# Router matmuls with the high and low weights side by side in one 32-column stationary operand

## The reference, cut to what matters

```python
logits = jnp.einsum('bsd,ed->bse', hidden_states, gate_w)      # 512 x 256 by 16 x 256, in each batch
scores = jax.nn.softmax(logits, axis=-1).transpose(0, 2, 1)
topk_w, topk_idx = jax.lax.top_k(scores, cap)                  # cap = 64 tokens of each expert
...
g = jnp.einsum('becd,efd->becf', x_tok, Wg)
u = jnp.einsum('becd,efd->becf', x_tok, Wu)
h = jax.nn.gelu(g, approximate=False) * u
eo = jnp.einsum('becf,edf->becd', h, Wd) * topk_w[..., None]
...
shared = jnp.einsum('bsf,df->bsd', jax.nn.gelu(gs, approximate=False) * us, Ws_d)
```

## Time and profile before

| | |
|---|---|
| time, median of 3 runs | 2467.9 us (2467.69 to 2471.45) |
| span of the profiled execution | 2465.3 us |
| phase A, to the last router matmuls | about 1268 us of it |
| TensorE busy | 96% |
| VectorE busy in phase A, by slices of the page | mostly 6 to 8 tenths |

### The profile page before, as it was taken

One profiled execution on the slowest core, in us unless ns is written; L12 is line 12 of the kernel. 1 busy time (PEld: TensorE's weight loads), 2 busy tenths in 40 slices (PEclk: granted clock), 3 DMA queues, 4 the chain that ended last, 5 costly groups with the idle time before them and its releaser, 6 DMA issues.

```text
span 2465.3 us, 40995 instructions
## 1 busy us (share of the span) xinstructions
PE 2372.3 (96%) x14388; PEld 2086.3 (85%) x14388; DVE 1567.9 (64%) x3198; ACT 1032.8 (42%) x1912; POOL 1150.4 (47%) x997
## 2 busy tenths in 40 slices
PE   6999999999998999999987999999999999999997
PEld 5888888888887888888876888888888888888886
DVE  6677767778776877788846455555554545555553
ACT  3545545444553545545442333333333333333332
POOL 1233333333332333333352666666666666666664
PEclk9999999999998999999998999999999999999999
DMA  2111111111111111111115444443444444434433
GB/s 90 53 44 59 51 60 60 52 51 57 54 61 44 60 43 60 52 60 60 59 62 90 86 90 82 88 84 66 79 84 87 86 85 88 84 60 86 84 62 43
DMA packets 78506, 167.03 MB, mean 68 GB/s; under 512 B 11744, under 2 KB 46720, under 8 KB 78368
## 3 DMA queue, kind: packets, MB, share of 16 engines
q0 software_dynamic: 49152, 67.14, 16.7%
q1 hardware_dynamic: 29216, 97.85, 11.8%
HBM read 97.71 MB, written 67.24 MB: 67 GB/s over the span
## 4 chain that ended last, share of the span: by engine, by line
PE 84%; DVE 6%; issue 4%; POOL 2%; DMA 1%; ACT 1%; SPq 0%; DVEq 0%; POOLq 0%; ACTq 0%
PE ps L349 26%; PE ps L351 26%; PE ps L350 26%; PE ps L501 2%; DVE stage L856 2%; PE ps L387 1%; DVE bn_stats L758 1%; PE ps L420 1%; DMA stage<-in_wd 1%; DVE x_t L753 1%; PE ps L442 1%; DVE hidden L753 1%; POOL rstd L1144 1%; POOL out L1209 1%; ACT x_t L693 0%
## 5 line engine op out<-in xcount | busy, mean ns | idle before, releaser
L349 PE MATMUL ps<-x_t,weights 128*128 128x512 f32 x1536 | 617.3, 402 | 23.2 <-DVE hidden_f L1111 13.3
L350 PE MATMUL ps<-x_t,weights 128*128 128x512 f32 x1536 | 602.5, 392 | 0.0
L351 PE MATMUL ps<-x_t,weights 128*128 128x512 f32 x1536 | 601.8, 392 | 0.0
L1209 POOL DMA_INDIRECT out<-x_rows,step_token x256 | 418.1, 1633 | 333.9 <-DVE x_rows L1090 275.4
L349 PE MATMUL ps<-weights,hidden 128*128 128x256 f32 x1536 | 435.8, 284 | 8.7 <-POOL hidden L1148 5.6
L351 PE MATMUL ps<-weights,hidden 128*128 128x256 f32 x1536 | 436.1, 284 | 0.0
L350 PE MATMUL ps<-weights,hidden 128*128 128x256 f32 x1536 | 436.0, 284 | 0.0
L1111 DVE TENSOR_TENSOR hidden_f<-gelu,ps 128x512 f32<-128x512 f32 x256 | 175.7, 686 | 379.0 <-ACT gelu L733 348.1
L733 ACT ACTIVATE gelu<-ps 128x512 f32<-128x512 f32 x256 | 152.8, 597 | 535.8 <-PE ps L351 508.4
L349 PEld LDWEIGHTS ps<-x_t,weights 128*128 128x128 f32 x1536 | 290.6, 189 | 83.6 <-DVE hidden_f L1111 13.5
L1148 POOL TENSOR_TENSOR hidden<-hidden_f,hidden 128x512 fp32r<-128x512 f32 x128 | 165.5, 1293 | 408.7 <-ACT hidden L647 408.7
(11 more groups left out here) (174 smaller groups left out, 4436.9 us busy)
## 6 DMA issues: line engine op xcount, KB each, us to landing
x_rows<-in_x SPq DMA_DIRECT2D x32, 512.0 KB, 3.5
pairs<-mod_rows SPq DMA_DIRECT2D x32, 512.0 KB, 4.3
h_rows<-stage SPq DMA_DIRECT2D x32, 512.0 KB, 2.6
out<-y_rows SPq DMA_DIRECT2D x32, 512.0 KB, 2.9
stage<-in_wg SPq DMA_DIRECT2D x16, 512.0 KB, 3.4
stage<-in_wd SPq DMA_DIRECT2D x16, 512.0 KB, 4.4
stage<-in_wu SPq DMA_DIRECT2D x16, 512.0 KB
x_rows<-h_rows,step_token POOLq DMA_INDIRECT x256
```

The lines of the kernel that those rows point to most:

```text
L349: pe.matmul(o, lhs(HI), rhs(HI), start=start, stop=False)
L350: pe.matmul(o, lhs(HI), rhs(LO), start=False, stop=False)
L351: return pe.matmul(o, lhs(LO), rhs(HI), start=False, stop=stop)
L1209: pool.indirect_dma_start(out=out_rows, out_offset=bass.IndirectOffsetOnAxis(ap=ICUR[g][:, t:t + 1], axis=0), in_=X1[:, g % 2, t * D:(t + ...
```

## The change

The router weights are laid out so that the 16 HI and the 16 LO columns of one half of the features are neighbours. One matmul with these 32 stationary columns gives HI weights by HI rows in PSUM rows 0 to 15 and LO weights by HI rows in rows 16 to 31; a second one with the 16 HI columns adds HI weights by LO rows to rows 0 to 15. There are four router matmuls a batch in place of six. The logits' copy and the four transposes then carry 32 rows, and VectorE adds the two groups with a reduction of its own into a new SBUF tile `GLS`, waits for it, and takes the maximum and the difference from `GLS`, not from PSUM.

```diff
--- before.py
+++ after.py
@@ -69,7 +69,7 @@
         V = sb("v", [P, 2, T, D], F32R)
         ROTK = sb("rot_k", [P, 2, KD, P], F32R)
         ROTV = sb("rot_v", [P, 2, KD, P], F32R)
-        GW = sb("gate_w", [P, 2, KD, E], F32R)
+        GW = sb("gate_w", [P, KD, 2, E], F32R)
         H1_T, H2_T = XT
         HID = H[0]
         A_T = H[1]
@@ -124,7 +124,8 @@
         NSQ = sb("norm_squares", [P, T])
         FAC = sb("out_factor", [P, T])
         GMX = sb("gate_max", [P, T])
-        GLT = sb("gate_logits_t", [E, S])
+        GLT = sb("gate_logits_t", [2 * E, S])
+        GLS = sb("gate_logits_sum", [P, T, E])
         GL = sb("gate_logits", [P, T, E])
         GEX = sb("gate_exp", [P, T, E])
         GS = sb("gate_sum", [P, T])
@@ -169,8 +170,8 @@
         st2, mv2, ve2, rs2, cent2, h2_ready, h2_stored = map(
             sem, ("st2", "mv2", "ve2", "rs2", "cent2", "h2_ready", "h2_stored"))
         h2t_done, h2t_hi, h2t_lo = map(sem, ("h2t_done", "h2t_hi", "h2t_lo"))
-        gate_done, gate_read, gate_t_done, gmax_ready, gl_ready, gexp_done, gsum, grs, sg_ready = map(
-            sem, ("gate_done", "gate_read", "gate_t_done", "gmax_ready", "gl_ready", "gexp_done", "gsum", "grs", "sg_ready"))
+        gate_done, gate_read, gate_t_done, gls_ready, gmax_ready, gl_ready, gexp_done, gsum, grs, sg_ready = map(
+            sem, ("gate_done", "gate_read", "gate_t_done", "gls_ready", "gmax_ready", "gl_ready", "gexp_done", "gsum", "grs", "sg_ready"))
         gu_done, gelu_done, mul_done, hid_hi, hid_lo = map(
             sem, ("gu_done", "gelu_done", "mul_done", "hid_hi", "hid_lo"))
         down_done, y_read, y_ready, y_stored = map(sem, ("down_done", "y_read", "y_ready", "y_stored"))
@@ -449,15 +450,17 @@
                 for k in range(KD):
                     wait(pe, h2t_hi, n * KD + k + 1)
                     wait(pe, h2t_lo, n * KD + k + 1)
-                    mm = mm3(PD[0:E, 512:512 + S], lambda a: GW[:, a, k, :], lambda a: H2_T[:, a, k, :],
-                             k == 0, k == KD - 1)
+                    pe.matmul(PD[0:2 * E, 512:512 + S], GW[:, k, :, :].rearrange("p a e -> p (a e)"),
+                              H2_T[:, HI, k, :], start=k == 0, stop=False)
+                    mm = pe.matmul(PD[0:E, 512:512 + S], GW[:, k, HI, :], H2_T[:, LO, k, :],
+                                   start=False, stop=k == KD - 1)
                 mm.then_inc(gate_done, 1)
 
             def gate_transposes(n):
                 wait_apart(pe, gate_read, n + 1)
                 for t in range(T):
-                    mm = pe.transpose(PD[:, 512 + t * E:512 + (t + 1) * E], GLT[:, t * P:(t + 1) * P],
-                                      IDENT[0:E, 0:E])
+                    mm = pe.transpose(PD[:, 512 + t * 2 * E:512 + (t + 1) * 2 * E], GLT[:, t * P:(t + 1) * P],
+                                      IDENT[0:2 * E, 0:2 * E])
                 mm.then_inc(gate_t_done, 1)
 
             def gate_up(n, fc):
@@ -698,7 +701,7 @@
                 if valid(i - 1):
                     act.wait_ge(gate_done, i)
                     wait(act, gate_t_done, i - 1)
-                    act.copy(GLT[:, :], PD[0:E, 512:512 + S]).then_inc(gate_read, 1)
+                    act.copy(GLT[:, :], PD[0:2 * E, 512:512 + S]).then_inc(gate_read, 1)
                     hidden(i - 1, 0)
                 if valid(i):
                     squares(i, (0, 1))
@@ -820,8 +823,8 @@
 
             def gate_weights():
                 dve.wait_ge(gate_in, 16)
-                link(dve.tensor_copy(GW[:, HI, :, :], GWF[:, :, :]))
-                split_lo(GW[:, LO, :, :], GWF[:, :, :], GW[:, HI, :, :]).then_inc(gw_ready, 1)
+                link(dve.tensor_copy(GW[:, :, HI, :], GWF[:, :, :]))
+                split_lo(GW[:, :, LO, :], GWF[:, :, :], GW[:, :, HI, :]).then_inc(gw_ready, 1)
 
             def modulations():
 
@@ -924,10 +927,12 @@
 
             def gate_max(n):
                 dve.wait_ge(gate_t_done, n + 1)
-                logits = PD[:, 512:512 + T * E].rearrange("p (t e) -> p t e", t=T)
-                dve.tensor_reduce(GMX[:, :], logits, AX.X, ALU.max).then_inc(gmax_ready, 1)
+                dve.tensor_reduce(GLS[:, :, :], PD[:, 512:512 + T * 2 * E].rearrange("p (t a e) -> p t e a", t=T, a=2),
+                                  AX.X, ALU.add).then_inc(gls_ready, 1)
+                dve.wait_ge(gls_ready, n + 1)
+                dve.tensor_reduce(GMX[:, :], GLS[:, :, :], AX.X, ALU.max).then_inc(gmax_ready, 1)
                 dve.wait_ge(gmax_ready, n + 1)
-                dve.tensor_tensor(GL[:, :, :], logits, GMX[:, :].unsqueeze(2).to_broadcast((P, T, E)),
+                dve.tensor_tensor(GL[:, :, :], GLS[:, :, :], GMX[:, :].unsqueeze(2).to_broadcast((P, T, E)),
                                   ALU.subtract).then_inc(gl_ready, 1)
 
             def gate_scores(n):
```

## The result

| | before | after |
|---|---|---|
| median of 20 runs each | 2469.05 us (2464.49 to 2473.12) | 2477.35 us (2470.6 to 2487.84) |
| span of the profiled execution | 2465.3 us | 2475.0 us |

The changed kernel is slower: ratio 1.0035, 95% interval [1.0025, 1.0045], +8.3 us between the medians. The prediction said +19.0. The sign is right and the time lies in the range, but the size is less than half. What was forecast inside the batches came nearly to the digit; about 12 us came back elsewhere. In the changed kernel L388 are the transposes of the normed rows (L387 before), L859 the normalisation (L856), L873 the hidden product (L870), L930 the new sum, L933 the maximum (L928), L935 the difference (L930), L964 the first MAX8 (L959), L1153 GpSimd's subtraction (L1148).

What follows compares the result with a forecast made beforehand. In batches 10 to 29 VectorE has no slack and its delays reach TensorE, whose saving a stop absorbs. +20.3 for the held difference less 1.3 for removed matmuls is +19.0 us: 2486.9 us median, range 2471 to 2492.

Steps and rivals of the forecast that it cites:

- L387 stops: TensorE's waits at the next batch's row transposes, forecast to grow from 0.46 to about 0.90 us in batch 14.
- L930 held under L1148: VectorE's difference, now with two SBUF inputs, waits out GpSimd's subtraction; next MAX8 1.01 us later, 1.10 in batches 26 to 29.
- The +20.3: Cost of the held difference in 20 batches: 16 x 1.01 plus four x 1.10 us, less 0.3 for TensorE's own time.
- 20 x 0.14: Extra 2.9 us in 20 batches if the difference began only at the recorded end of GpSimd's subtraction.
- The first: Rival: VectorE's difference is not held, its zero-step input differing; only the reduction is paid, +4.9 us, 2472.8 us; chance 0.11.
- The second: Rival: TensorE's saving gets past the next rows' transposes, 32 x 0.44 = 14.1 us less, 2453.8 us; chance 0.04.
- The third: Rival: VectorE's maximum, now from SBUF, is held as well, 20 x 0.24 = 4.8 us more, 2491.7 us; chance 0.04.
- The fourth: Rival: two stops in each of 20 batches lower TensorE's clock; 40 us on top if half do, 2527 us; chance 0.03.
- The fifth: Rival: saving and addition both vanish in overlooked VectorE slack, 2466 to 2468 us; chance 0.04.
- the row of L877: VectorE's similar two-SBUF-input operation, ending 0.02 us after GpSimd's subtraction; from it the difference was put 0.08 us after.
- the term for the removed matmuls: On TensorE: 0.44 us saved a batch, swallowed in batches 1 to 29, counting only in 0, 30 and 31: 1.3 us.
- Phase B unchanged to 1 us: Expectation for the profile after: the second phase of the kernel keeps its time to within 1 us.

Runs made afterwards that it cites:

- e3: The kernel before with two of six router matmuls left out (the products with the LO weights), nothing added; 2458.59 us, ratio 0.9950 to the kernel before.
- e6: The changed kernel with GpSimd's addition to `y_rows` (L1183) moved behind its power for `out_norm`; 2429.29 us, ratio 0.9859 to the kernel before.
- e5: The kernel before with GpSimd's addition to `y_rows` (L1183) moved behind its power for `out_norm`, SyncE's store behind the modulation load; 2445.59 us, ratio 0.9912.
- e1: The changed kernel with the sum written to PSUM, so the difference again has one input in PSUM; 2466.52 us, ratio 0.9988 to the kernel before.
- e7: The changed kernel with maximum and difference behind L873 of quarter 1, `a_times_v(.., 1)` waiting for the sum; 2454.69 us, ratio 0.9946 to the kernel before.
- e2: The kernel before, six router matmuls, plus a copy of the logits to SBUF that maximum and difference read; 2487.76 us, ratio 1.0075.
- e9: The kernel before with 16 tiny matmuls (recorded as 32) in TensorE's set-up; 2463.98 us, ratio 0.9983 to the kernel before.
- e4: The changed kernel run once more without an edit; 2476.06 us, ratio 1.0023 to the kernel before.
- e10: The changed kernel with two tiny matmuls (recorded as four) ahead of each batch's router matmuls; 2481.44 us, ratio 1.0061 to the kernel before.
- e12: The changed kernel with one tiny matmul (recorded as two) ahead of each batch's router matmuls; 2487.59 us, ratio 1.0072 to the kernel before.
- e11: The changed kernel with 12 tiny matmuls (recorded as 24) in the set-up, nothing in the loops; 2484.3 us, ratio 1.0065 to the kernel before.
- e8: The changed kernel with GpSimd's addition late and maximum and difference behind L873 of quarter 1; 2423.73 us, ratio 0.9831 to the kernel before.

## Why the prediction was off

**Right, with its size.** The forecast was L387 stops of 0.9 us in batches 1 to 29, and the waits show 29 of up to 0.9. The saving on TensorE was put at 0.44 us a batch and worth nothing in batches 1 to 29; 0.46 is what the timeline shows, e3 leaves the periods as they were to 0.04 us, and e6 against e5 shows 0.45 once the stop is away. The sum was put at 0.32 us to the next start (measured 0.32), L930 held under L1148 with an end 0.08 us behind it (0.08), the period about 39.2 us in batches 10 to 24 (39.23) and 38.07 in 1 to 8 (38.07 to 38.09 in 2 to 7, 37.92 in 1 and 8, where it was 37.91 before), the stop at gate_up(2) about 1.0 us (up to 1.0, 20 times). The +20.3 measured 18.9 in the trace without batch 17, 19.9 with 1.0 assumed for it. Two small slips of the working change nothing: an element of a reduction costs 1.02 ns by the two rows, not 1.03, and 20 x 0.14 is 2.8 us, not 2.9. e1 (difference from PSUM) and e7 (difference behind L873) take the hold away by two ways, e2 adds it alone.

**The rivals.** The first (not held) fell by the 0.92 us; a zero-step operand in SBUF counts as a second SBUF input. The second (the saving passes L387) fell by e3's periods; the faster runs of e3 are not its mechanism, since they come from batch 17 and phase B. The third (the maximum held too) fell: 220 ns. The Trainium skill (page "SBUF — State Buffer", section "Who interferes with whom") says that tensor_reduce never contends on this chip, and the 220 ns agree. The fourth (the clock falls at the new stops) fell: the clock is 1.00 in batch 14 with stops of 0.92 and 0.89 us, and no stretch of half clock is recorded in batches 10 to 29 but the one in batch 17. The fifth (nothing moves) fell with the periods of batches 10 to 24. The rule of the Trainium skill on the same page and in the same section, that the lock is exclusive and the second to issue waits, taken to the letter with a start at L1148's recorded end, would give 2.8 us more; the row of L877 was the better guide.

**The step that failed** is the term for the removed matmuls: "It counts only in batches 0, 30 and 31: 3 x 0.44 = 1.3 us gained", and with it "Phase B unchanged to 1 us". The term measured about 11 us (e3: 11.3, by its interval 9 to 16). It was worked out from the time that the matmuls take on the engine. They also take up places in TensorE's list, and all behind them moves up: at the outer loop's turn in batch 17 the second stop of 2.4 us and, in this profile, 13.7 us at half clock vanish (batch 17 is 6.1 us shorter with its own hold in it, and 6.1 in e9, which has none), and in phase B part of the loop's turns need no loading (3.9 us in the profiled execution, 8.4 in e4's). Shown by e9, which moves batch 17 alone by 6.1 us without touching any work, and by e10 to e12, which bring back the loading in phase B, e12 with the second stop as well, each with the changed router in it. e11 has nothing added inside the loops: against after, batch 17 is 5.9 us longer, batch 30 1.3 and the part from batch 31 on 5.7. That the loading is what TensorE waits for is read from the packets that go with the stops; no run takes the loading away by itself. The view that could have warned was there before: the page's row of 110 instruction packets, and the waits on "issue". A rival "the turns of the loops cost something else once the list has another length", with both signs and some 10 us, was missing.

**What stays open.** First, which turn is spared its loading. In the seven profiles with the short list (after, e1, e3, e4, e6, e7, e8) 3, 3, 3, 0, 1, 3 and 3 of the six jumps back in phase B's loop load the list anew, and not the same ones; e4 and after are the same program. In the seven others (before, e2, e5, e9 to e12), whose loop stands between 8 recorded matmuls ahead of its old place and 32 behind it, all six do. So the list decides whether a turn can be spared, and something that differs from one execution to the next decides whether it is. Five turns of e4 without a packet show that the loop can be held whole in one place of the list; whether it touches one packet more in the others isn't recorded. That the changed kernel's runs spread over 17 us and those of before over 9 would fit this; it isn't shown.

Second, what in the list makes the stops of batch 17. By the count of e11, all four kernels with the second stop have the outer loop at its old place, and no other has; e10 and e11 both start it 12 matmuls behind and yet take 46.6 and 52.2 us, so its start alone doesn't decide, and the place of its end (20 and 4 matmuls behind the old one) was not tried by itself.

Third, how the stop makes the length of the low clock: a first step of 5.11 us (after) was followed by 3.4 us at half clock, 5.17 (e9) by 6.8, 5.18 (e1) and 5.23 (e7) by 13.7, 5.50 (e10) by 3.4, 6.62 (e11) by 17.1, and 5.62 with a second stop of 2.43 (before) by 17.1, 6.71 with one of 2.20 (e12) by 13.7.

## What to carry to other kernels

An intermediate result that VectorE reads twice is better left in PSUM, or its reader with two SBUF inputs kept out of GpSimd's elementwise work: the place of a 64-column tile decided over 0.7 us in each of 20 batches. A saving on the bounding engine is worth nothing while a later stop on the same engine absorbs it; take that stop away first (e5), then the same two matmuls are worth 0.45 us a batch (e6), and with the hold moved too the kernel gains 1.7% (e8). For changes of under half a per cent in a kernel with loops, count the instructions added to and removed from each engine's list, and test with the list padded to its old length before believing the work's own price.

## What the runs showed of the hardware

16 matmuls of six columns in the set-up made the kernel before 0.17% faster (e9), 12 made the changed one 0.3% slower (e11, 1.0065 against 1.0035), one a batch 0.37% (e12, 1.0072): the place of the loops in the list was worth up to 9 us here. A 6-column matmul whose operands aren't rounded to float32r was recorded as two instructions. A turn of phase B's loop with 9 instruction packets took 1.3 us longer than one with one (142.0 and 140.7 us). VectorE's four normalisations, each with one 256-column tensor in SBUF and two columns of scalars beside it, took 3.46 us where GpSimd's 2.40 us addition had begun just before them, and 1.38 us without it (e5). The first of the four bore all of it: 2.48 us before and 2.49 after, ending 0.14 to 0.15 us behind the addition, while the other three took 0.40 us each as in e5.
